# float32r halves for a low-rank adapter in a conditioned feed-forward kernel on one core

## What is computed

```python
# layer 0: a gated feed-forward block, conditioned by a scale per feature
scale = cond @ norm_w.T + 1.0
h = x * (scale[:, None, :] * rsqrt(mean(x * x) + EPS))
val, gate = split(h @ up_w.T)                 # up_w (4096, 512)
h = val * gelu(gate)
x1 = act_quant(h) @ weight_quant(down_w).T + x   # down_w (512, 2048)
# layer 1: an adapter whose weights depend on the condition
Wd_b = Wd + ((cond @ Wdd.T + bdd) * 0.1).reshape(B, 128, 512)
Wu_b = Wu + ((cond @ Wdu.T + bdu) * 0.1).reshape(B, 512, 128)
down = relu(einsum('bld,bnd->bln', x1, Wd_b) + bd)
out = x1 + einsum('bln,bdn->bld', down, Wu_b) + bu
```

## Time and profile before

| | |
|---|---|
| median of 3 runs | 993.27 us (992.75 to 993.3) |
| profiled execution, its own time | 991.73 us |
| its span, first to last instruction | 989.6 us |
| mean granted TensorE clock | 0.992 |
| busy: PE, DVE, ACT, POOL | 962.7, 649.3, 444.4, 53.7 us |
| last up product of the main part starts | 890.94 us |
| first adapter product (L1055) | 898.59 us |
| chunk loop starts (down layer of chunk 2) | 934.22 us |

### The profile page before, as it was taken

The page is one execution under the profiler, slowest core; times in us unless marked ns, Lnnn a source line. Parts: engine busy times, 40 slices in busy tenths (PEclk is TensorE's granted clock), DMA queues, the critical chain, the costliest instruction groups (busy, mean ns, idle before and its releaser), DMA issues.

```text
span 989.6 us, 13640 instructions
## 1 busy us (share of the span) xinstructions
PE 962.7 (97%) x5281; PEld 467.4 (47%) x5311; DVE 649.3 (66%) x1028; ACT 444.4 (45%) x823; POOL 53.7 (5%) x52
## 2 busy tenths in 40 slices
PE   6999989999999999999999999999999999997998
PEld 4555434444444444444444444444444444443553
DVE  5878678756776578656875678566875674338333
ACT  5888557312762257322751266214741265115222
POOL 1000000000000000000000000000000000004254
PEclk9999989999999999999999999999999999999999
DMA  9335443444534443443444434443444434012464
GB/s 329 139 128 167 135 150 114 133 140 122 158 109 129 148 131 115 151 134 109 139 138 138 135 126 124 128 139 113 142 139 118 149 107 117 33 54 86 165 231 178
DMA packets 73305, 134.59 MB, mean 136 GB/s; under 512 B 5268, under 2 KB 10904, under 8 KB 72728
## 3 DMA queue, kind: packets, MB, share of 16 engines
q1 hardware_dynamic: 73240, 133.72, 42.4%
HBM read 112.72 MB, written 20.97 MB: 135 GB/s over the span
## 4 chain that ended last, share of the span: by engine, by line
PE 93%; DVE 3%; DMA 1%; issue 1%; ACT 1%; SPq 0%; POOL 0%; DVEq 0%; POOLq 0%
PE bank L899 22%; PE bank L900 22%; PE bank L901 22%; PE bank L956 11%; PE bank L911 6%; PE bank L1070 3%; PE bank L1055 2%; PE bank L872 1%; PE bank L882 1%; PE bank L1046 1%; DVE h L838 1%; DVE delta_reg L677 1%; DMA delta_reg<-in_L_cond_Wdd 0%; DMA xn<-in_x 0%; PE bank L936 0%
## 5 line engine op out<-in xcount | busy, mean ns | idle before, releaser
L899 PE MATMUL bank<-x_split,w_hi 128*128 128x512 f16 x1024 | 389.8, 381 | 2.2 <-DVE x_split L640 2.2
L900 PE MATMUL bank<-x_split,w_hi 128*128 128x512 f16 x1024 | 389.5, 380 | 0.0
L901 PE MATMUL bank<-x_split,w_lo 128*128 128x512 f16 x1024 | 389.2, 380 | 0.0
L677 DVE STREAM_TRANSPOSE delta_reg<-delta_reg 128x512 f32<-128x512 f32 x256 | 258.8, 1112 | 27.7 <-PE bank L911 22.8
L515 ACT ACTIVATE g<-h 128x512 f32<-128x512 f32 x128 | 80.6, 630 | 306.2 <-DVE h L746 306.2
L899 PEld LDWEIGHTS bank<-x_split,w_hi 128*128 128x128 f16 x1024 | 100.5, 98 | 128.4 <-issue 14.3
L901 PEld LDWEIGHTS bank<-x_split,w_lo 128*128 128x128 f16 x1024 | 100.5, 98 | 121.8 <-issue 1.6
L746 DVE SCALAR_TENSOR_TENSOR h<-bank,desc,g 128x512 f32<-128x512 f32 x128 | 92.6, 723 | 96.4 <-issue 72.0
L900 PEld LDWEIGHTS bank<-x_split,w_hi 128*128 128x128 f16 x1024 | 100.5, 98 | 112.7 <-issue 1.1
L504 ACT ACTIVATE g<-bank,desc 128x512 f32<-128x512 f32 x128 | 87.4, 683 | 124.0 <-PE bank L901 123.8
L956 PE MATMUL bank<-wqT,qreg 128*128 128x512 bf16 x482 | 111.4, 379 | 1.6
(11 more groups left out here) (124 smaller groups left out, 576.9 us busy)
## 6 DMA issues: line engine op xcount, KB each, us to landing
delta_reg<-in_L_cond_Wdd SPq DMA_DIRECT2D x64, 512.0 KB, 3.6
delta_reg<-in_L_cond_Wdu SPq DMA_DIRECT2D x64, 512.0 KB, 3.7
qreg<-in_L_cond_up_w SPq DMA_DIRECT2D x32, 256.0 KB, 4.3
xr<-in_x SPq DMA_DIRECT2D x32, 256.0 KB, 4.3
x_scratch<-xr SPq DMA_DIRECT2D x32, 256.0 KB, 4.7
xn<-in_x SPq DMA_DIRECT2D x7, 1024.0 KB, 6.4
out_y<-w_hi SPq DMA_DIRECT2D x7, 1024.0 KB, 4.3
h<-in_L_cond_down_w SPq DMA_DIRECT2D x4, 1024.0 KB, 7.9
```

What stands on the lines that cost most here:

```text
L677: last = dve.transpose(natT[:, t, kk, :, :].rearrange("p a (r e) -> p e a r", e=4), nat[:, u % NAT, kk, :])
L899: pe.matmul(bank[:, :], w_hi[:, k, cols], xh[:, par, k, :], start=(k == 0), stop=False)
L900: pe.matmul(bank[:, :], w_hi[:, k, cols], xl[:, par, k, :], start=False, stop=False)
L901: mm = pe.matmul(bank[:, :], w_lo[:, k, cols], xh[:, par, k, :], start=False, stop=(k == KD - 1))
```

## The change

float32r is a four-byte type that TensorE reads at reduced precision. The adapter no longer multiplies f32 tiles. Each of x1, the ReLU's output and the two weight matrices of a batch is held as two float32r tiles, the rounded value (hi) and what it lacks (lo), and each f32 product is replaced by hi*hi + hi*lo + lo*hi into the same bank. To make the halves:

- weights: VectorE writes the sum into the scratch tile s_bc, copies it to hi and subtracts hi into lo, each step waiting for the one before (`layer_of_batch`);
- x1: ScalarE's copy out of PSUM writes x1_hi; VectorE subtracts it from the bank into x1_lo (`x1_lower`), and only then may the bank be filled again;
- ReLU: ScalarE runs it twice, into down_hi and down_f32, and VectorE subtracts (`down_lower`).

The order in the ramp changes too: chunk 1's x1 is transposed in one piece after the scales, its copies stand behind `copy_scales`, and VectorE's subtractions are put among the quantising steps. The halves lie in the space of w_hi, w_lo and delta_reg, where x1T, out_buf, down_T, wd_all and wu_all lay. GpSimd's and SyncE's programs are not changed.

```diff
@@ ScalarE
             def copy_x1(c, par, slices=range(KD)):
...
-                    act.activation(x1T[:, par, k, :], x1_bank[k][:, :], ACT.Copy).then_inc(x1T_done, 1)
+                    act.activation(x1_hi[:, par, k, :], x1_bank[k][:, :], ACT.Copy).then_inc(x1T_done, 1)
             def relu_down(c, par):
                 act.wait_ge(down_full, c + 1)
-                if not (c < 2):
+                if c >= 2:
                     act.wait_ge(up_full, TT * (c - 1))
-                act.activation(down_T[:, par, :], TA[:, :], ACT.Relu, bias=bdc[:, 0:1]).then_inc(relu_done, 1)
+                    act.wait_ge(down_split, c - 1)
+                for half in (down_hi, down_f32):
+                    act.activation(half[:, par, :], TA[:, :], ACT.Relu, bias=bdc[:, 0:1]).then_inc(relu_done, 1)
...
             copy_x1(0, 0)
-            copy_x1(1, 1, (0, 1))
             copy_scales(NCH - 1)
-            copy_x1(1, 1, (2, 3))
+            copy_x1(1, 1)
             round_tiles(0, 1)
             relu_down(0, 0)
             round_tiles(1, 4)
@@ VectorE
             def layer_of_batch(b):
-                dve.wait_ge(delta_turned, 2 * b + 1)
-                dve.scalar_tensor_tensor(wd_all[:, b, :], HY[:, :], DELTA_SCALE, base_wd[:, :],
-                                         ALU.mult, ALU.add).then_inc(layers_ready, 1)
-                dve.wait_ge(delta_turned, 2 * b + 2)
-                dve.scalar_tensor_tensor(wu_all[:, b, :], TB[:, :], DELTA_SCALE, base_wu[:, :],
-                                         ALU.mult, ALU.add).then_inc(layers_ready, 1)
+                for i, (turned, base_w, hi, lo) in enumerate((
+                        (HY[:, :], base_wd[:, :], wd_hi[:, b, :], wd_lo[:, b, :]),
+                        (TB[:, :], base_wu[:, :], wu_hi[:, b, :], wu_lo[:, :, b, :]))):
+                    dve.wait_ge(delta_turned, 2 * b + i + 1)
+                    if b + i > 0:
+                        dve.wait_ge(layers_split, 2 * b + i)
+                    dve.scalar_tensor_tensor(s_bc[:, :], turned, DELTA_SCALE, base_w, ALU.mult, ALU.add).then_inc(layers_ready, 1)
+                    dve.wait_ge(layers_ready, 2 * b + i + 1)
+                    dve.tensor_copy(hi, s_bc[:, :]).then_inc(layers_hi, 1)
+                    dve.wait_ge(layers_hi, 2 * b + i + 1)
+                    if i == 0:
+                        dve.tensor_tensor(lo, s_bc[:, :], hi, ALU.subtract).then_inc(layers_split, 1)
...
+            def x1_lower(c, par, slices=range(KD)):
+                for k in slices:
+                    dve.wait_ge(x1T_done, KD * c + k + 1)
+                    dve.tensor_tensor(x1_lo[:, par, k, :], x1_bank[k][:, :], x1_hi[:, par, k, :], ALU.subtract).then_inc(x1_split, 1)
+
+            def down_lower(c, par):
+                dve.wait_ge(relu_done, 2 * c + 2)
+                dve.tensor_tensor(down_lo[:, par, :], down_f32[:, par, :], down_hi[:, par, :], ALU.subtract).then_inc(down_split, 1)
...
             finish_max(NCH - 1)
+            x1_lower(0, 0)
             dve.wait_ge(s_bc_done, NCH)
-            for k in range(0, FT - 6, 2):
-                quantise_last(k)
+            quantise_last(0)
+            quantise_last(2)
+            x1_lower(1, 1)
+            down_lower(0, 0)
+            quantise_last(4)
+            quantise_last(6)
+            down_lower(1, 1)
+            quantise_last(8)
             add_up(0, 0, (0, 1))
-            quantise_last(FT - 6)
+            quantise_last(10)
             add_up(0, 0, (2, 3))
-            quantise_last(FT - 4)
+            quantise_last(12)
             add_up(1, 1, (0, 1))
-            quantise_last(FT - 2)
+            quantise_last(14)
             add_up(1, 1, (2, 3))
+            x1_lower(2, 0)
             for t in range(TT):
                 residual(NCH - 1, t, last_bank[t % 2])
             for c in range(2, NCH):
+                down_lower(c, c % 2)
+                if c + 1 < NCH:
+                    x1_lower(c + 1, (c + 1) % 2)
                 add_up(c, c % 2)
@@ TensorE
...
                     if not is_first(c):
-                        pe.wait_ge(x1T_done, KD * (c - 1) + k + 1)
+                        pe.wait_ge(x1_split, KD * (c - 1) + k + 1)
...
             def down_layer(c, b, par):
-                pe.wait_ge(layers_ready, 2 * b + 2)
-                pe.wait_ge(x1T_done, KD * (c + 1))
+                pe.wait_ge(layers_split, 2 * b + 2)
+                pe.wait_ge(x1_split, KD * (c + 1))
                 if not is_first(c):
-                    pe.wait_ge(relu_done, c)
+                    pe.wait_ge(relu_done, 2 * c)
                 for k in range(KD):
-                    mm = pe.matmul(TA[:, :], wd_all[:, b, k * BN:(k + 1) * BN], x1T[:, par, k, :], start=(k == 0), stop=(k == KD - 1))
+                    cols = slice(k * BN, (k + 1) * BN)
+                    pe.matmul(TA[:, :], wd_hi[:, b, cols], x1_hi[:, par, k, :], start=(k == 0), stop=False)
+                    pe.matmul(TA[:, :], wd_hi[:, b, cols], x1_lo[:, par, k, :], start=False, stop=False)
+                    mm = pe.matmul(TA[:, :], wd_lo[:, b, cols], x1_hi[:, par, k, :], start=False, stop=(k == KD - 1))
                 mm.then_inc(down_full, 1)
             def up_layer(c, b, par):
-                pe.wait_ge(relu_done, c + 1)
+                pe.wait_ge(down_split, c + 1)
...
-                    pe.matmul(up_bank[t][:, :], down_T[:, par, t * P:(t + 1) * P],
-                              wu_all[:, b, :],
-                              start=True, stop=True).then_inc(up_full, 1)
+                    rows = slice(t * P, (t + 1) * P)
+                    pe.matmul(up_bank[t][:, :], down_hi[:, par, rows], wu_hi[:, b, :], start=True, stop=False)
+                    pe.matmul(up_bank[t][:, :], down_hi[:, par, rows], wu_lo[:, :, b, :], start=False, stop=False)
+                    pe.matmul(up_bank[t][:, :], down_lo[:, par, rows], wu_hi[:, b, :], start=False, stop=True).then_inc(up_full, 1)
 
             turn_x1(0, 0, 0)
             turn_absrun(NCH - 1)
-            turn_x1(1, 0, 1, (0, 1))
             spread_scales(NCH - 1)
-            turn_x1(1, 0, 1, (2, 3))
+            turn_x1(1, 0, 1)
             down_layer(0, 0, 0)
             down_layer(1, 0, 1)
```

More of the change, by code:

```diff
@@ L8 @@
 BF16 = mybir.dt.bfloat16
+F32R = mybir.dt.float32r
 I32 = mybir.dt.int32
@@ L52, in sem @@
             return ctx.enter_context(nc.semaphore(name))
[L55 to L58, removed]
         wqT = sb("wqT", [P, FT, D], BF16)
@@ L74, in conditioned_block @@
         s_bc = sb("s_bc", [P, CH], F32)
-        delta_reg = sb("delta_reg", [P, NAT + NATT, 1024], F32)
-        nat = delta_reg[:, 0:NAT, :].rearrange("p s (k e) -> p s k e", k=2)
-        natT = delta_reg[:, NAT:, :].rearrange("p s (k a m) -> p s k a m", k=2, a=HB)
         stage = sb("stage", [P, 512], F32)
@@ L112, in conditioned_block @@
         bdc = sb("bdc", [P, 1], F32)
+        with (nc.sbuf_tensor("delta_reg", [P, NAT + NATT, 1024], F32) as delta_reg,
+              nc.sbuf_tensor("w_hi", [P, KD, 2 * FF], F16) as w_hi,
+              nc.sbuf_tensor("w_lo", [P, KD, 2 * FF], F16) as w_lo):
+            pass
+        wd_lo = sb("wd_lo", [P, NB, D], F32R)
+        wu_lo = sb("wu_lo", [P, KD, NB, BN], F32R)
+        wd_hi = sb("wd_hi", [P, NB, D], F32R)
+        wu_hi = sb("wu_hi", [P, NB, D], F32R)
+        x1_hi = sb("x1_hi", [P, 2, KD, CH], F32R)
+        out_buf = sb("out_buf", [P, 2, TT, D], F32)
+        x1_lo = sb("x1_lo", [P, 2, KD, CH], F32R)
+        down_hi = sb("down_hi", [P, 2, CH], F32R)
+        down_lo = sb("down_lo", [P, 2, CH], F32R)
+        down_f32 = sb("down_f32", [P, 2, CH], F32)
+        nat = delta_reg[:, 0:NAT, :].rearrange("p s (k e) -> p s k e", k=2)
+        natT = delta_reg[:, NAT:, :].rearrange("p s (k a m) -> p s k a m", k=2, a=HB)
         bank = [ctx.enter_context(nc.psum_tensor(f"bank{i}", [P, 512], F32)) for i in range(8)]
@@ L143, in conditioned_block @@
         x1_buf = [xn, x_split[:, 0, :].rearrange("p (t d) -> p t d", t=TT)]
-        x1T = w_hi_reg[:, 0:2 * KD * CH].rearrange("p (a k t) -> p a k t", a=2, k=KD)
-        out_buf = w_hi_reg[:, 2 * KD * CH:].rearrange("p (a t d) -> p a t d", a=2, t=TT)
-        down_T = w_lo_reg[:, 0:2 * CH].rearrange("p (a t) -> p a t", a=2)
         delta_d = delta_reg[:, 0:2, :].rearrange("p s e -> p (s e)").rearrange("p (b d) -> p b d", b=NB)
         delta_u = delta_reg[:, 2:4, :].rearrange("p s e -> p (s e)").rearrange("p (k b n) -> p k b n", k=KD, b=NB)
-        wd_all = delta_reg[:, 4:6, :].rearrange("p s e -> p (s e)").rearrange("p (b c) -> p b c", b=NB)
-        wu_all = delta_reg[:, 6:8, :].rearrange("p s e -> p (s e)").rearrange("p (b d) -> p b d", b=NB)
         x1_bank = [GATE[0], VAL[0], GATE[1], VAL[1]]
@@ L181, in conditioned_block @@
             "nat_turned", "delta_mm", "stage_full", "stage_free"))
-        delta_back, delta_turned, layers_ready = (sem(n) for n in ("delta_back", "delta_turned", "layers_ready"))
```

(21 more changed lines are left out.)

## The result

The changed kernel takes 1004.02 us (median of 4 runs, 1003.31 to 1004.91) against 993.07 us before: 1.1% slower, ratio 1.0111 with a 95% interval of 1.0093 to 1.0129. Its profiled execution took 1004.12 us, with a span of 1002.1 us against 989.6.

A forecast was written before the change was run, and what follows sets the result against it. TensorE was taken as the bound, with 93% of the chain of waits. Profiled 991.73 us plus loop 1.4, last chunk -0.2, ramp 8.1, weights 1.8, clock 1.5 gave 1004.3; with 1.54 median offset 1005.9 us, range 1000 to 1014.

The forecast's parts named there:

- VectorE's order in the loop and in the ramp: Main case, chance 0.80: VectorE's order sets both parts, float32r products take one pass; 1000 to 1014 us.
- The loop: Adapter's chunk loop: closed chain through VectorE takes 9.09 us a chunk against 8.81; five periods cost +1.4 us.
- The ramp: Before the chunk loop: ten more VectorE operations, nearly all on its path, up to the transposes of chunk 2; +8.1 us.
- That stays: In the ramp, quantising steps 0 and 2 still take 7.5 us, because POOL adds the bias at the same time.
- The second wait for the ReLU: In the ramp, VectorE idles 2.2 us before the second ReLU subtraction, while ScalarE rounds step 6 and runs two ReLUs.
- The weights: Adapter weight batches 1 to 3: serial copies and subtractions delay TensorE's second transposes 0.58 us each; +1.8 us.
- The clock: After idle in the ramp, 1.2 GHz exposed at chunk 2's transposes and first main down products; one loss, +1.5 us.
- A product at 0.43 us: Rival, chance 0.10: a product of halves costs 0.43 us throughout the adapter, loop period 12.3 us; 1029 us in all.
- That TensorE remains the pace: Rival, chance 0.05: VectorE's added work fits beside TensorE in loop and ramp, 13.5 us saved; 981.6 us.
- the loop would run at TensorE's own length: No-change rival, chance 0.04: loop period 6.93 us gives back 9.4 us, eaten by ramp and weights; 993.8 us.
- the end: Last chunk, with no x1 behind it: 7.9 us to the last addition against 8.14; counted as -0.2 us.

The follow-up runs named there:

- e1_bank: Changed kernel with the fourth up product in x1's first bank from chunk 2 on, so not waiting for the second addition; 997.7 us, 1.0048 of before.
- e8_pool_short: Kernel before, with POOL adding the bias to only 8 of 512 columns in chunk 1; 991.01 us against 992.6, ratio 0.9988.
- e2_weights: Changed kernel with both weight sums of a batch made before the copies and subtractions; 1003.54 us, ratio 1.0111.
- e3_ramp_f32: Changed kernel with f32 products, single copies and the old order for chunks 0 and 1, halves from chunk 2 on; 998.12 us, ratio 1.0056.
- e4_all: Changed kernel with e1_bank, e2_weights and e3_ramp_f32 in one; 987.77 us, ratio 0.9948.
- e7_pipe2: e4_all with the next down layer and later transposes ahead of each up layer, more buffers, earlier x1 loads, additions reordered; 987.08 us, ratio 0.9948.

## Why the prediction was right

It said 1005.9 us in 1000 to 1014; measured were 1004.02. The sign came out of the step that it rested on, VectorE's order in the loop and in the ramp. That the size is so near is in part luck, as its errors partly cancelled.

- **The loop.** VectorE's order closes the period over five subtractions and two additions. e1_bank shows it by giving that one wait another bank: 9.38 us a period become 7.9, and the whole is 6.3 us shorter. The period was 9.38 us, not 9.09. Two sizes were off. A product of halves stands 0.228 us after its predecessor, not 0.216, so a down layer is 2.74 us. And the follower of a product that has waited comes later still; the forecast had left this out. The timeline of the changed kernel:

```profile
952.15 0.19 PEld L1112 LDWEIGHTS bank<-wu_hi,down_hi 128*128 128x128 f32 x1 [1.68 <-DVE out_buf L860]
952.15 0.50 PE L1112 MATMUL bank<-wu_hi,down_hi 128*128 128x512 f32 x1 [1.26 <-DVE out_buf L860]
952.26 0.19 PEld L1113 LDWEIGHTS bank<-wu_lo,down_hi 128*128 128x128 f32 x1
952.49 0.40 PE L1113 MATMUL bank<-wu_lo,down_hi 128*128 128x512 f32 x1
```

The waiting product's weight load begins with it (952.15), the next one's 0.23 us ahead (952.26), and the two products stand 0.34 us apart instead of 0.23. Fifteen products at 0.012 us more and these 0.11 are the 0.29 us by which the period was missed. Five periods, from down layer to down layer (943.72 to some 990.6), cost 2.9 us instead of 1.4.
- **The ramp.** Forecast +8.1, measured +5.7. The step that failed was "That stays": the 7.5 us of steps 0 and 2, with POOL beside them. The timeline of the changed kernel:

```profile
902.86 3.64 PE L1084 MATMUL bank<-identf,x_split 128*128 128x128 f32 x16 [1.25 <-DVE x_lo L718]
...
904.43 1.28 DVE L865 TENSOR_TENSOR h<-h,s_bc 128x512 f32<-128x512 f32 x2
...
906.59 5.72 POOL L440 TENSOR_TENSOR out_buf<-x_split,bu_bc 128x512 f32<-128x512 f32 x4 [4.49 <-PE bank L1084]
...
907.17 1.50 DVE L867 TENSOR_SCALAR qreg<-h 128x512 bf16<-128x512 f32 x1
...
908.60 2.47 DVE L718 TENSOR_TENSOR x_lo<-bank,x_hi 128x512 fp32r<-128x512 f32 x4
...
911.61 1.25 DVE L722 TENSOR_TENSOR down_lo<-down_f,down_hi 128x512 fp32r<-128x512 f32 x1 [0.54 <-ACT down_f L577]
```

Chunk 1's transposes waited for the subtractions and then ran at the lower clock, 3.64 us for 1.91. POOL's second round began at 906.59, when steps 0 and 2 were nearly over (904.43 to 908.60, 4.2 us). It met one rounding (1.50) and one ReLU subtraction (1.25, against 0.69 alone); between them VectorE was subtracting from PSUM, where the four took 2.47 us as if alone. So steps 0 and 2 were 3.3 us cheaper than forecast, and 1.1 us came back behind them: 0.54 idle and 0.56 in the ReLU's subtraction. With 0.3 less for chunk 0's subtractions that is the miss of 2.4 us. POOL's round was moved by the change, not ended, and what is left of the meeting in this ramp was not tried; e8_pool_short prices it in the ramp of before.
- **The second wait for the ReLU** in the ramp came as worked out: VectorE idle 2.18 us ahead of the second subtraction (forecast 2.2), TensorE idle 4.83 us ahead of the fourth up product.

```profile
918.12 0.69 DVE L722 TENSOR_TENSOR down_lo<-down_f,down_hi 128x512 fp32r<-128x512 f32 x1 [2.18 <-ACT down_f L577]
...
921.60 0.79 PE L1112 MATMUL bank<-wu_hi,down_hi 128*128 128x512 f32 x1 [4.83 <-DVE out_buf L860]
```

- **The weights.** Forecast +1.8; 0.63 us for each of three batches, 1.9, and gone in e2_weights. TensorE's own wait was 0.41 us:

```profile
861.19 0.65 PE L966 MATMUL bank<-identf,delta_reg 128*128 128x128 f32 x4 [0.41 <-DVE s_bc L705]
```

The other 0.2 us lie in the restart of the transposes behind it; they were not looked at singly.
- **The clock.** 1.5 us were counted for the main down products; they took 13.95 us against 13.75, so next to nothing. TensorE did work at 1.2 GHz in the ramp (granted clock 0.50 from 902 to 908 and from 919 to 925 us), but nearly all of it beside VectorE's work: what shows is within the 0.54 us for which VectorE stood ahead of 911.61, behind chunk 1's transposes, a first down layer that ended at 910.3 us, and the ReLUs. The cost that had not been seen lies at the other end: 2.1 us of idle before the last up layer, after which the clock was down in the profiles of e1_bank, e2_weights and e3_ramp_f32, at 1.3 us, and up in those of the changed kernel and of e4_all.
- **The rivals.** A product at 0.43 us is out by its rows: the products stand 0.23 us apart, and each weight load, 0.19 us, lies beside the product before it. That TensorE remains the pace, or that the loop would run at TensorE's own length, is out for this order of work; e7_pipe2 shows that the second is to be had by another, at 7.39 us with the dearer product.

The errors partly cancelled. The ramp was put 2.4 us too high and the clock 1.4 (from the transposes of chunk 2 to the loop it was 15.85 us against 15.79); the loop was put 1.5 us too low, the weights 0.1 and the end 0.3: -0.2 was forecast, and from the last down layer (990.62 us) on it was 11.45 us against 11.33. Together that is 1.9 us, the distance between forecast and measurement. For the profiled execution 1004.3 us was forecast and 1004.12 came: the same 1.9 us too many, made up by the first chunk's +1.9, which no term of the sum holds. That was luck.

## What to carry to other kernels

Splitting an operand moves work from the engine that is full to those that make the halves, so price the splitting, and write down the closed chain of one period with every engine's order in it: here the cheaper products lost 1.1%, about half of it in the ramp, where VectorE was full already, and a good quarter in the loop, where five subtractions stood ahead of an addition that freed a bank. One bank given otherwise turned the loop's 9.38 us a chunk into 7.9, below the 8.81 of before. Use the cheap form only where its engine is the bound: halves in the loop and f32 in the ramp, with that bank and with both weight sums first, were 0.5% faster than the kernel before; without those two repairs (e3_ramp_f32) they were still 0.6% slower. A shorter loop shows at the end only if nothing at its ends, the last load, the last ReLU, the last stores, takes the place of what was saved.

## What was not expected of the hardware

- A float32r product of 512 columns cost about a quarter of an f32 one, 0.228 us against 0.858, so that three cost 0.69; it stood 0.012 us further behind its predecessor than a 16-bit one. Its weight load is 0.19 us long at full clock (952.15; 202 ns on average on L1112) against 0.098. Whether the load causes the difference was not tried.
- The copy to float32r on VectorE, 0.43 us, and the subtractions with a float32r result, 0.68 us, cost what f32 ones cost.
- The same 2.08 us of idle before the last up layer left the clock at 2.4 GHz in two profiled executions (the changed kernel, e4_all) and was followed by 1.2 GHz in three (e1_bank, e2_weights, e3_ramp_f32). What decides between them is open.
- VectorE's operation on two SBUF operands, 0.69 us alone, took 1.25 and 1.62 us beside POOL's addition, while four subtractions out of PSUM beside it took 2.47 us, as without it.
